# Expert rows for the second matrix side by VectorE's block transpose instead of TensorE's

## The reference

```python
x = _layernorm(x + attn(x, w_q, w_k, w_v, w_o))
x = _layernorm(x + xattn(x, ctx, ctx, Wq, bq, Wk, bk, Wv, bv))
gate = softmax(xf @ gate_w + gate_b); topv, topi = top_k(gate, 2); topv = topv / topv.sum(-1)
for each expert e: out += (relu(xf @ w1[e] + b1[e]) @ w2[e] + b2[e]) * combine[:, e]   # w1: 256 x 1024
x = _layernorm(x + out)
```

## Time and profile before

| | |
|---|---|
| median of 3 runs | 1423.28 us (1423.0 to 1425.81) |
| the profiled execution's own time | 1436.35 us |
| its span, mean granted clock of TensorE | 1433.8 us, 0.993 |
| busy: TensorE, weight loads, VectorE, ScalarE, GpSimd | 96%, 70%, 73%, 60%, 42% |
| chain that ended last | TensorE 76%, VectorE 7%, issue 5%, DMA 5%, GpSimd 3% |

### The profile page before, as it was taken

The page is one execution under the profiler, slowest core; times in us unless marked ns, Lnnn a source line. Parts: engine busy times, 40 slices in busy tenths (PEclk is TensorE's granted clock), DMA queues, the critical chain, the costliest instruction groups (busy, mean ns, idle before and its releaser), DMA issues.

```text
span 1433.8 us, 48738 instructions
## 1 busy us (share of the span) xinstructions
PE 1382.5 (96%) x18474; PEld 997.0 (70%) x18474; DVE 1044.6 (73%) x1928; ACT 866.2 (60%) x1964; POOL 596.1 (42%) x1051
## 2 busy tenths in 40 slices
PE   9999999999999999999999989989889999999995
PEld 5455455577777664466554458878879999999995
DVE  6888888888888888789899836756545555555563
ACT  4688888878888877778787764442223333333331
POOL 3221212223222333631225414676665556565564
PEclk9999999999999999999999999999999999999998
DMA  6226555444533323323423251222232222222221
GB/s 211 78 87 193 157 160 171 127 115 122 141 109 120 96 72 98 115 71 81 151 62 91 73 194 49 75 90 90 90 109 75 75 75 75 71 73 74 68 80 54
DMA packets 108912, 147.65 MB, mean 103 GB/s; under 512 B 28075, under 2 KB 80618, under 8 KB 107658
## 3 DMA queue, kind: packets, MB, share of 16 engines
q1 hardware_dynamic: 94026, 104.92, 25.4%
q0 software_dynamic: 14080, 38.32, 8.2%
q10 hardware_dynamic: 576, 1.31, 0.3%
HBM read 81.43 MB, written 63.04 MB: 101 GB/s over the span
## 4 chain that ended last, share of the span: by engine, by line
PE 76%; DVE 7%; issue 5%; DMA 5%; POOL 3%; ACT 1%; SPq 1%; another core or an unknown queue 0%; POOLq 0%; DVEq 0%; ACTq 0%
PE pa L1014 14%; PE pb L1014 13%; PE pa L1267 13%; PE po L1193 13%; PE pb L1281 11%; PE px L1014 7%; DVE neg L1569 3%; DMA out<-space,y_tags 2%; PE pb L1007 1%; DMA space<-y_parts,y_tags 1%; DMA attention_out<-space 1%; PE po L1128 1%; POOL y_parts L959 1%; POOL x_by_expert L852 1%; PE px L1007 1%
## 5 line engine op out<-in xcount | busy, mean ns | idle before, releaser
L1569 DVE TENSOR_REDUCE neg<-pa 128x1 f32<-128x1024 f32 x512 | 611.7, 1213 | 66.8 <-PE pa L1014 53.0
L1392 ACT ACTIVATE w_sb<-pb 128x512 f32<-128x512 f32 x996 | 589.0, 598 | 113.5 <-PE pb L1014 74.2
L1014 PE MATMUL pb<-w_sb 99*32 99x512 bf16 x3984 | 418.8, 381 | 6.0 <-ACT w_sb L1392 3.2
L1498 ACT ACTIVATE space<-pa,b1T_sb 128x128 f32<-128x128 f32 x568 | 154.4, 382 | 339.5 <-PE pa L1267 288.3
L1014 PE MATMUL pa<-w_sb 96*32 96x512 bf16 (+1 forms) x4208 | 337.0, 380 | 5.3 <-DVE neg L1569 3.8
L1193 PE MATMUL po<-w_sb,space 128*32 128x256 f32 x4000 | 316.3, 379 | 0.2
L1267 PEld LDWEIGHTS pa<-xgT,attn_t 128*128 128x128 f32 x2272 | 267.4, 193 | 17.1 <-ACT xgT L1437 7.6
L1267 PE MATMUL pa<-xgT,attn_t 128*128 128x128 f32 x2272 | 271.4, 277 | 7.7 <-DVE attn_t L1904 4.0
L1281 PE MATMUL pb<-w_sb,space 128*128 x1136 | 263.4, 383 | 0.0
L1281 PEld LDWEIGHTS pb<-w_sb,space 128*128 128x128 f32 x1136 | 210.9, 192 | 26.1 <-issue 0.3
L1014 PEld LDWEIGHTS pa<-w_sb 96*32 96x32 bf16 (+1 forms) x4208 | 129.3, 97 | 107.9 <-DVE neg L1569 30.9
(11 more groups left out here) (252 smaller groups left out, 1209.5 us busy)
## 6 DMA issues: line engine op xcount, KB each, us to landing
y_parts<-attn_t SPq DMA_DIRECT2D x13, 896.0 KB, 4.9
w_sb<-w SPq DMA_DIRECT2D x17, 512.0 KB, 4.5
attention_out<-space SPq DMA_DIRECT2D x64, 128.0 KB
w_sb<-w SPq DMA_DIRECT2D x7, 1024.0 KB, 7.6
xg<-x_by_expert SPq DMA_DIRECT2D x54, 130.0 KB
q_parts<-w_sb SPq DMA_DIRECT2D x48, 128.0 KB, 3.2
w_sb<-q_parts SPq DMA_DIRECT2D x64, 96.0 KB
w_sb<-k_parts SPq DMA_DIRECT2D x64, 96.0 KB
```

What stands on the lines that cost most here:

```text
L1014: mm = pe.matmul(out[at:end], lhsT[:, at:end], rhs, start=start, stop=stop, tile_position=(0, at))
L1392: act.activation(ex_of(n)[:, half * HALF:(half + 1) * HALF], score_bank(n, half), ACT.Exp, scale=SCALE).then_inc(e_done, 1)
L1498: ins = act.activation(hT[tile % 2][:, f, :], pH[tile % 2][:, f, :], ACT.Relu, bias=g.b1_sb[:, bass.ds(e * FT + f, 1)])
L1569: dve.tensor_reduce(neg[i % 2][:, t:t + 1], pa[n % 2][:, :], AX.X, ALU.max, negate=True).then_inc(max_done, 1)
```

## The change

- Every tile's rows are loaded twice. The second load, `load_blocks`, brings them in 32x32 block order: four DMAs per tile, each to 32 partitions, four runs of 64 words in each, into one of three rooms (`stages`; a fourth serves tile 1 only). VectorE's transpose of 128x256, which turns each 32x32 block, gives `xgT` directly; the 256 dimensions come out in another order, so w1's rows are put into that order on the host, and `xgT` is read as four runs of 32.
- TensorE's transposes, the bank `pX` and ScalarE's `copy_x` are gone. Some waits for banks go with them.
- `load_blocks` of tile t+3 and `load_xg` of tile t+2 are issued in turn t, in this order. `xg` has three buffers, `y_tag` four, `keep(t)` stands in turn t. `load_blocks` waits only for `x_taken` (for tiles 3 and 4 also for `last_rep`).
- Gathered results lie in three buffers (the third is `o_last` made 128 high). `gather(2)` waits for `last_rep`.
- In turns with tokens ScalarE copies both halves of w1, and VectorE turns behind the statistics instead of behind the w1 copies. Two semaphores are merged into one.

```diff
-    XS = 4
-    TAGS = 6
+    XS = 3
+    YS = 3
+    BLOCK = 32
+    TAGS = 4
...
+        stages = [fold[:, 0:2, :, :].rearrange("p b k c -> p (b k c)")[:, 0:D], cv_room[:, 0:D], cv_room[:, D:2 * D], xg[2][:, 0:D]]
+        flat_xT = [sb(f"xgT{i}", [P, KD * P]) for i in range(2)]
+        xgT = [room[:, :].rearrange("p (t k c) -> p k t c", k=KD, c=BLOCK) for room in flat_xT]
...
-        x3 = [spaces[2][:, (2 + i) * D:(3 + i) * D] for i in range(2)]
+        x3 = [spaces[2][:, (2 + i) * D:(3 + i) * D] for i in range(2)] + [o_room[:, :]]
...
+                def load_blocks(tile):
+                    row = number(sp, tile, 0)
+                    if tile >= 2:
+                        sp.wait_ge(x_taken, max(tile - 2, 1))
+                    if tile in (3, 4):
+                        sp.wait_ge(last_rep, 4)
+                    settle(sp, g.settled_dma)
+                    at = stage(tile)[0]
+                    for a in range(P // BLOCK):
+                        cols = slice(a * KD * BLOCK, (a + 1) * KD * BLOCK)
+                        sp.dma_start(stages[at][a * BLOCK:(a + 1) * BLOCK, :].rearrange("p (t c) -> p t c", c=KD * BLOCK),
+                                     g.xe_dram[bass.ds(row, P), cols].rearrange("(t p) c -> p t c", p=BLOCK)
+                                     ).then_inc(blocks_in[at], 16)
...
                     if tile >= XS:
                         sp.wait_ge(kept, tile - XS + 1)
-                        sp.wait_ge(turned_x, tile - XS + 1)
                         sp.wait_ge(c_both, tile - XS + 1)
...
                         sp.wait_ge(scored, 2 * TB)
-                        for tile in range(XS):
+                        for tile in range(2):
+                            load_blocks(tile)
+                        for tile in range(2):
                             load_xg(tile)
...
-                    if 0 < tile <= FFN_TILES - XS:
-                        if tile - 1 + XS == EARLY:
+                    if tile + 3 < FFN_TILES:
+                        if tile + 3 == EARLY:
...
-                        load_xg(tile - 1 + XS)
+                        load_blocks(tile + 3)
+                    if tile + 2 < FFN_TILES:
+                        load_xg(tile + 2)
...
-                    if tile >= 2:
-                        pool.wait_ge(out_rows, 16 * (tile - 1))
+                    if tile == 2:
+                        pool.wait_ge(last_rep, 4)
+                    if tile >= YS:
+                        pool.wait_ge(out_rows, 16 * (tile - YS + 1))
...
-                    if tile + 2 < FFN_TILES:
-                        if MAIN_PROJ < j < NT:
-                            pe.wait_ge(added, j + 1)
-                        turn_x(tile + 2)
...
-                    if tile + 2 < FFN_TILES:
-                        copy_x(tile + 2)
...
+                    if with_tokens(tile):
+                        copy_late_w1(tile + 2, 0)
...
+                def turn_x(tile):
+                    at, loads = stage(tile)
+                    dve.wait_ge(blocks_in[at], 16 * P // BLOCK * loads)
+                    if tile >= 2:
+                        dve.wait_ge(up_done, tile - 1)
+                    dve.transpose(flat_xT[tile % 2][:, :], stages[at]).then_inc(x_taken, 1)
...
                     if tile + 2 < FFN_TILES and not with_tokens(tile):
                         copy_w1(tile + 2, 1, e)
+                        turn_x(tile + 2)
                     if tile:
                         residual(tile - 1)
                         measure_3(tile - 1)
+                    if with_tokens(tile):
+                        turn_x(tile + 2)
```

More of the change, by code:

```diff
@@ L213, in behind_step @@
         return s < len(steps) and steps[s] == name and tile_of(p)[1] is not None
-    def feeds(p):
-        turn, s = divmod(p, TURN)
-        return (0, 1).index(s) if turn == TURNS - 1 and s in (0, 1) else None
     LAST_TOKENS = TB + SHIFT
@@ L225, in with_tokens, with stage @@
         return MAIN_PROJ <= NT - TB + tile - SHIFT <= NT
+    def stage(tile):
+        if tile < 2:
+            return (0, 3)[tile], 1
+        turn, at = divmod(tile - 2, 3)
+        return at, turn + (2 if at == 0 else 1)
     def in_pa(n):
@@ L447, in stream @@
         xg_in = [sem(f"xg_in{i}") for i in range(XS)]
+        blocks_in = [sem(f"blocks_in{i}") for i in range(4)]
         y_out = [sem(f"y_out{i}") for i in range(TAGS)]
@@ L1072, in proj @@
                         pe.wait_ge(last_scaled, 2)
+                        if j == MAIN_PROJ + 1:
+                            pe.wait_ge(o_out, NH)
+                        else:
+                            pe.wait_ge(added, j)
                     else:
@@ L1443, in behind @@
                     b = next_batch(p)
-                    if feeds(p) is not None:
-                        copy_x(feeds(p))
-                    elif s == 0 and b:
+                    if s == 0 and b:
                         high_part(b, turn % TB)
@@ L1537, in _ @@
                     if with_tokens(tile):
-                        copy_late_w1(tile + 2)
+                        copy_late_w1(tile + 2, 1)
                     if MAIN_GATE <= j < NT:
@@ L1899, in side_taken @@
                         pick_rows()
+                    if turn == TURNS - 1 and s in (4, 5):
+                        turn_x(s - 4)
                 def copy_w1(tile, k, e):
@@ L1988, in last_sum @@
                     tile = FFN_TILES - 1
-                    own, other = y[tile % 2], x3[tile % 2]
+                    own, other = y[tile % 2], x3[tile % YS]
                     dve.wait_ge(result_done, tile + 1)
@@ L1996, in moments @@
                 def moments(tile):
-                    z = x3[tile % 2]
+                    z = x3[tile % YS]
                     dve.wait_ge(c_sum, tile + 1)
@@ L2012, in _ @@
                 copy_w1(1, 0, e)
-                keep(0)
-                keep(1)
                 norm_1(MAIN_PROJ)
@@ L2025, in _ @@
                         dve.wait_ge(table_2, len(TABLE_2))
-                    if tile + 2 < FFN_TILES:
-                        e = number(dve, tile + 2, 1)
-                        keep(tile + 2)
+                    keep(tile)
                     if LAST_TOKENS + 1 < tile < FFN_TILES - 1:
@@ L2035, in _ @@
                         cross_rec(j - 1)
-                    if tile + 2 < FFN_TILES:
+                    if tile + 2 < FFN_TILES and not with_tokens(tile):
+                        e = number(dve, tile + 2, 1)
                         copy_w1(tile + 2, 0, e)
```

70 lines of the change are left out of this document (26 added, 44 removed).

## The result

| | before | after |
|---|---|---|
| median of 4 runs each, us | 1424.4 | 1398.55 (1397.5 to 1401.5) |
| the profiled execution's own time, us | 1436.35 | 1397.69 |
| its span, mean granted clock | 1433.8, 0.993 | 1395.7, 0.994 |

The ratio is 0.9823, with a 95% interval of 0.9804 to 0.9842: 25.85 us faster by the medians. The forecast was 1400.4 and 22.9 us. The profiled executions differ by 38.7 us, 13 more than the medians; the first experiment shows where those 13 belong.

A forecast was written before the change was run, and what follows sets the result against it. TensorE, busy 96% of the span, was taken as the bound, with GpSimd pacing turns 13 to 23. Terms -11.4 - 2 - 1 - 14 + 1.5 gave -26.9; keeping 10 of the 14, -22.9: 1400.4 us, range 1391 to 1413.

The forecast's parts named there:

- TensorE's transposes, -11.4: All tiles: TensorE loses 142 transposes, 0.21 us a pair, where it is full: -11.4 us.
- Turns 0 to 6 and the attention part, -1.9: Seven transpose pairs in turns 0 to 6 and two in the last attention pairs, with TensorE full: -1.9 us.
- ScalarE's copy waits, -2 and -1: TensorE's waits behind ScalarE's copy of turned rows go: -2 us late, -1 for two earlier waits.
- Three result buffers and looser loads, -14, of which I kept 10: Turns 13 to 23: gathers stop waiting for a free result buffer, 94.2 to 80 us; -14, cut to 10 for unprofiled runs.
- Small pieces, +1.5: Block loads, 512 pieces of 256 B per tile, make gathers wait behind them on the DMA engines: +1.5 us in all.
- VectorE's transpose, 0.45 us: Each tile's 128x256 f32 transpose on VectorE takes 0.45 us, hidden in a quiet turn with 2 us to spare.
- The attention part, 0: Six more SyncE issues before the last head's maxima are stored: taken as 0, ends 0 and 3 us.
- the middle term: Turns 13 to 23: the third result buffer ends the gathers' wait; -14 us, of which 10 were kept.
- Only TensorE's share: Rival: late rows give way to another wait, or runs lacked the long waits; 1411 us, chance 0.20.
- The ring: Rival: small pieces delay gathers in the gather-to-gather chain, binding at 3.8 us; 1437 us, chance 0.07 shared with slower operand reads.
- that rival: TensorE reads block order more slowly in the ups: 25 us given back, about 1424; chance 0.07 shared with delayed gathers.
- my signs of being wrong: Ups over 3.57 us, gather to residual over 4, TensorE waiting for VectorE's transpose or w1 copies, turns near 7.2.

The follow-up runs named there:

- the first experiment, b_again: The kernel before, unedited, run and profiled a second time: 1425.65 us, ratio 1.0002 to before.
- turns_again: The changed kernel with two 128x128 transposes per turn given back to TensorE, into unused columns: 1409.69 us, ratio 0.9891 to before.
- third_only: The kernel before with only the third buffer for gathered results added: 1411.23 us, ratio 0.9901 to before.
- two_results: The changed kernel with two buffers for gathered results instead of three: 1415.84 us, ratio 0.9937 to before.
- whole_rows: The changed kernel with the second load as one DMA of whole rows instead of four in block order: ratio 0.98 to before, on the slower chip.
- token_again: The changed kernel with tile 23's token load issued from ScalarE's queue instead of SyncE's: 1393.37 us, ratio 0.9786 to before.
- the later group: Runs in which the unedited changed kernel was measured again beside the kernel before: 1399.41 us, ratio 0.9825.
- both: The changed kernel with tile 23's token load on ScalarE's queue and variance plus epsilon added by VectorE instead of GpSimd: 1389.25 us, ratio 0.9748 to before.

## Why the prediction was right, point by point

*TensorE's transposes, -11.4.* Late, -9.5: measured -9.6 (318.8 to 309.2), and turns_again gives it back. Turns 0 to 6 and the attention part, -1.9: **this part failed.** The step said that TensorE is as full there as late, by a window with 68.5 busy us of 69. Turns 1 to 6 take 58.05 us, before 58.16. TensorE was full, and turns 1 to 4 did get 0.8 us shorter in all. But turns 5 and 6 got 0.7 us longer: there TensorE now waits 1.6 us for VectorE's chain behind the output rows, to which the change added a transpose, and 0.5 in b_again. Busy time that includes the work to be removed doesn't say who is next. In turn 0 the transposes are 0.2 of 1.1 us, the rest is the clock (see turns_again).

*ScalarE's copy waits, -2 and -1.* Late, a median turn of b_again is 7.245 us and its 44 add up to 318.8, so on the faster chip there was nothing to gain; the 2.7 us were of the first profile (321.3). They aren't in the difference of the medians. Nor are the 2.4 us around turns 11 and 12: b_again has no TensorE wait for ScalarE's copy at all from 850 us on. The 0.5 us that turns 7 to 12 lose are TensorE's transposes (0.2 us each in turns 9, 11 and 12). So this term was nothing, for a forecast of 3.

*Three result buffers and looser loads, -14, of which I kept 10.* Measured -12.9 against the first profile and -15.7 against b_again; 81.3 us, forecast 80, and 5.1 us idle ahead of the gathers of tiles 13 to 23, forecast near 5. The mechanism is shown from both sides by third_only and two_results. Some 4.4 of the 15.7 us are the clock, by an estimate: TensorE worked for 8.7 us at the lower level in these turns of b_again (from 1005.0 and 1033.6 us on), and for none in the changed kernel. The cut to 10 was wrong: I laid the 13 us between profile and median into this stretch. Of the 9.3 us between the spans of the two profiles of before, 6.8 lie ahead of S(0), 4.2 in turns 7 to 12 and 2.5 in the late turns, while turns 13 to 23 were even 2.8 shorter in the first, and turn 0 and the end 1.4. I had also given the looser order under 1 us; beside the buffer it and the rest of the change give about 4.

*Small pieces, +1.5.* They had 13 to 53 ns each in the bounds; it is 22 (16828 packets more than in the earlier trace rows for 11.8% of 200 us x 16), the DMA share 0.36, and TensorE's quiet turn has no trace of it. For turns 7 to 12 whole_rows leaves up to 3.4 us open. The rule of the Trainium skill that I had set against the change ("DMA: Bandwidth & Descriptors", section "Bandwidth") would have put the share near 0.75 (the page's times are of DMAs issued from GpSimd, these loads are issued by SyncE). By these rows a tile's four loads, 512 x 22 ns, take 11.3 us of one engine, 0.7 us of the 16, so its time for one transfer isn't time in which the engines are full.

*VectorE's transpose, 0.45 us.* 0.44:

```profile
L1855 DVE STREAM_TRANSPOSE xgT<-cv 128x256 f32<-128x256 f32 x18 | 7.9, 438 | 0.0
```

It starts in a quiet turn at 1207.10, where TensorE wants it at 1209.64: 2.1 us to spare, as forecast.

*The attention part, 0.* Against b_again up(0) starts 2.4 us sooner, and S(0) at the same 849.8 us: up(1) waits 7.05 us instead of 4.5 for a copy that hangs on SyncE's token load. So what was won ahead of it was lost in that wait; token_again wins it back. The block loads did not delay that token load: SyncE issues it at 844.39 us in b_again, at 844.91 and 843.89 in the two profiles of the changed kernel.

The sum against the median was -22.9 for a measured -25.85 (and -25.5 in the later group); with the full 14 it would have been -26.9. The profiles of b_again and the changed kernel, both of the faster kind, differ by 29.7 us: 9.6 late, 15.7 in turns 13 to 23, 0.5 in turns 7 to 12, 1.1 in turn 0, 0.1 in turns 1 to 6, 1.9 behind S(68), and some 0.8 outside these stretches. The 1.9 I had not forecast: 0.2 are transposes, 1.7 come behind the last matmul, where third_only has 1.5 of them too; in kernels with the same end this stretch varies by 2 us, so the cause stays open. (b_again's profiled execution lies 1.8 us over its median and that of the changed kernel 0.9 under.) So the early and the copy terms were too large by some 3 us (4.9 forecast, 1.7 measured), the middle term was too small by 5.7, the 1.5 us for the small pieces don't show in the turns that I had priced, and 1.9 had no term. That the total came within 3 us of the medians is in part luck: these errors stood against one another.

*The rivals.* "Only TensorE's share" would have been 11.4 + 1; the middle stretch was there in the unprofiled runs too, by third_only's 13.6 us. The ring never bound: TensorE waits for nothing in turns 24 to 67, and the idle time of GpSimd ahead of a late gather is 0.34 to 0.98 us. But my price for it was wrong. Gather to residual takes 4.06 us in the median of these 44 turns and up to 4.42, over 4 in 35 of them, where I had the ring bind at 3.8 and the gain gone at 4.4; the turn is 7.03 us all the same. In 43 of the 44 VectorE doesn't wait for the gather at all: the residual stands behind its w1 copy and its transpose, and third_only, without any small pieces, has 4.25. So that length isn't the gather's own. Up rows stayed at 3.57 us, so the block order costs TensorE nothing (and that rival's total should have been 1425: 1400.4 + 25). Of my signs of being wrong two showed beside this one. TensorE waits for VectorE's transpose, 3.0 us in three turns; it was GpSimd's pace under another name. And it waits for a w1 copy, 7.05 us at up(1), where it had waited 4.0 before; behind that stood the token load.

## What to carry to other kernels

When a wait names an engine or a load, follow it to the engine without idle time: here the same stall was called a load before, a transpose with two_results, and both times it was a gather waiting for a scatter to land. An order that is loosened ahead of such a wait only renames it; the buffer that the slow engine waits for pays, and the looser order pays after it. Before a term is trimmed because profile and median differ, take a second profile of the same kernel: the difference may lie in another stage, or come with another chip.

## What the runs showed that I had not expected

- Two chips run the kernel before in 1424.8 and 1424.9 us and a third in 1438.2 (medians of 17, 9 and 9 runs), at nearly the same granted clock and, in the kernel that was profiled on both kinds, the same length of instructions. The difference is in waits of the attention part and in turns 7 to 12; quiet turns without TensorE's transposes are 7.03 us on both kinds. Whether it is the chip or the occasion isn't shown.
- A 256-byte piece of the hardware queue takes 22 to 23 ns of one engine, not the 53 ns that the queue's mix of mostly 1040-byte rows had shown, nor a quarter of that.
- The granted clock fell with the waits: 0.94 from 966 to 1048 us in b_again and 1.00 in the changed kernel. In two_results the ups behind waits of 2.73, 2.94 and 3.83 us took 5.46 to 5.47 us instead of 3.84, with a granted clock of 0.72 from 1009 to 1015 us and from 1067 to 1073: these waits cost 1.6 us each beyond themselves. The one of 3.27 us did not bring it, nor did that of 0.78; in third_only one of 1.96 us did (granted clock 0.50 from 1041.6 to 1045.0 us). The changed kernel keeps one such fall, at up(1), and loses 1.7 us by it; token_again and `both` have none there.
